# A decoder's state space stage: every third state's product du x B on VectorE instead of GpSimd

## What is computed

```python
xz = x @ W_in
xc, r = jnp.split(xz, 2, axis=-1)
xs = causal_conv(xc, conv_w) + conv_b              # 4 taps
u = silu(xs)
dbc = u @ W_x
delta = softplus(dbc[..., :dtr] @ W_dt + b_dt)
Bm = dbc[..., dtr:dtr + n]                          # n = 16 states
Cm = dbc[..., dtr + n:]
deltaA = jnp.exp(jnp.einsum('bld,dn->lbdn', delta, A))
deltaBu = jnp.einsum('bld,bln->lbdn', delta * u, Bm)
h = dA * h + dBu                                    # along the 256 tokens
y = sum_n h[n] * c[n] + u * D
out = y * silu(r)
return out @ W_out + xs
```

## Time and profile before

| what | value |
|---|---|
| median of 3 runs | 3277.06 us (3275.04 to 3279.24) |
| the profiled execution | 3278.29 us |
| its span | 3276.5 us |
| TensorE busy over the span | 2911.2 us (89%) |
| VectorE busy | 2047.5 us (62%) |
| ScalarE busy | 1527.8 us (47%) |
| GpSimd busy | 1007.0 us (31%) |
| state space stage, first to last scan | 1883.9 to 2523.8 us |

### The profile page before, as it was taken

One profiled execution on the slowest core, in us unless ns is written; L12 is line 12 of the kernel. 1 busy time (PEld: TensorE's weight loads), 2 busy tenths in 40 slices (PEclk: granted clock), 3 DMA queues, 4 the chain that ended last, 5 costly groups with the idle time before them and its releaser, 6 DMA issues. The chain is left out here.

```text
span 3276.5 us, 51834 instructions
## 1 busy us (share of the span) xinstructions
PE 2911.2 (89%) x19136; PEld 1909.8 (58%) x19136; DVE 2047.5 (62%) x2551; ACT 1527.8 (47%) x2911; POOL 1007.0 (31%) x937
## 2 busy tenths in 40 slices
PE   7999688788888888869999899999985999989998
PEld 5666355434444444436666677777763556657776
DVE  4788544589999999670111099999998223324444
ACT  3444211288999998641221276666662111114443
POOL 0000044346666665430000067656666000000000
PEclk9999799889999999889999999999996999989999
DMA  2010322268888888640003111111113611200000
GB/s 87 27 39 26 106 62 69 56 132 168 157 169 168 169 169 181 154 158 14 26 26 125 46 46 53 52 52 52 46 46 101 100 35 38 65 20 14 26 26 27
DMA packets 497941, 256.57 MB, mean 78 GB/s; under 512 B 412112, under 2 KB 449616, under 8 KB 496208
## 3 DMA queue, kind: packets, MB, share of 16 engines
q1 hardware_dynamic: 487456, 247.66, 29.9%
q0 software_dynamic: 10288, 6.29, 1.3%
HBM read 121.65 MB, written 33.69 MB: 47 GB/s over the span
## 5 line engine op out<-in xcount | busy, mean ns | idle before, releaser
L1063 DVE TENSOR_REDUCE xh_top<-xh_seen 128x1 f32<-128x512 f32 (+1 forms) x768 | 632.1, 863 | 59.3 <-PE xh_seen L965 45.5
L1035 ACT ACTIVATE xh_prob<-xh_sc,xh_bias,xh_scale 128x1024 int16<-128x1024 f32 (+1 forms) x512 | 610.0, 1201 | 77.7 <-PE xh_sc L965 73.9
L1929 POOL TENSOR_TENSOR ss_state<-ss_du,ss_b_all 128x1024 f32<-128x1024 f32 x128 | 376.0, 2944 | 264.7 <-PE ss_turned L1649 188.1
L965 PE MATMUL xh_seen<-xh_kT,xh_qT 96*128 96x512 bf16 x1024 | 358.0, 392 | 78.4 <-DVE xh_top L1063 76.0
L1969 DVE TENSOR_TENSOR_SCAN ss_state<-ss_decay,ss_state 128x1024 f32<-128x1024 f32 x128 | 377.4, 2949 | 34.4 <-ACT ss_decay L1828 34.4
L965 PE MATMUL xh_sc<-xh_kT,xh_qT 96*128 96x512 bf16 x1024 | 314.2, 389 | 1.3 <-ACT xh_prob L1035 1.3
L1089 POOL CAST xh_probT<-xh_pairs 128x2048 int16<-128x2048 uint8 x128 | 241.8, 1889 | 17.2 <-DMA xh_pairs<-xh_prob 8.8
L1656 PE MATMUL ss_bank<-ss_xc,hold_w_conv 128*128 128x256 f32 x1024 | 237.7, 388 | 0.7 <-ACT ss_xc L1840 0.7
L965 PEld LDWEIGHTS xh_seen<-xh_kT,xh_qT 96*128 96x128 bf16 x1024 | 90.2, 98 | 240.4 <-DVE xh_top L1063 216.0
L1828 ACT ACTIVATE ss_decay<-ss_delta,ss_a 128x255 f32<-128x255 f32 x512 | 210.7, 496 | 25.9 <-DVE ss_state L1969 25.5
L1656 PEld LDWEIGHTS ss_bank<-ss_xc,hold_w_conv 128*128 128x128 f32 x1024 | 195.8, 195 | 29.0 <-ACT ss_xc L1840 1.1
(11 more groups left out here) (281 smaller groups left out, 4962.4 us busy)
## 6 DMA issues: line engine op xcount, KB each, us to landing
ss_b_all<-ss_states SPq DMA_DIRECT2D x8, 2048.0 KB, 7.2
xa_kT<-xp_kT SPq DMA_DIRECT2D x8, 768.0 KB, 6.0
xh_qT<-xa_qT SPq DMA_DIRECT2D x48, 128.0 KB, 3.3
xh_kT<-xa_kT SPq DMA_DIRECT2D x48, 128.0 KB, 3.3
sa_x<-in_x SPq DMA_DIRECT2D x8, 512.0 KB, 3.7
sa_y<-in_x SPq DMA_DIRECT2D x8, 512.0 KB, 4.7
x_after_self_attention<-sa_y_out SPq DMA_DIRECT2D x8, 512.0 KB, 3.0
xp_x<-x_after_self_attention SPq DMA_DIRECT2D x8, 512.0 KB, 6.6
```

The lines of the kernel that those rows point to most:

```text
L965: ins = pe.matmul(out[:, c * D:(c + 1) * D], qT[s][:, t * P:(t + 1) * P], kT[s][:, at + c * D:at + (c + 1) * D], start=True, stop=True)
L1035: act.activation(out, scores, ACT.Exp, bias=bias[t % RING][:, :], scale=scale[s][:, t:t + 1], accum_out=total[s][:, half, t:t + 1]).then_i ...
L1063: ins = v.tensor_reduce(top[t % RING][:, k:k + 1], scores[:, 0:n], AX.X, ALU.max)\
L1929: g.tensor_tensor(state[k % RING][:, :, :], du[s][:, :, :], spread(b_all[s][:, k, :], KD), ALU.mult)\
```

## The change

The products of states 2, 5, 8, 11 and 14 are issued by VectorE at the end of the slot before their scan; the other eleven stay on GpSimd in their slots. VectorE's products count on a semaphore of their own, `drive_there`, and the scans and SyncE's refill of `b_all` wait on the one or both that concern them. Everything else keeps its place.

```diff
@@ -1472,6 +1472,8 @@
     UNITS = 18
     DECAY_LEAD = 2
     DRIVE_LEAD = 3
+    BY_VECTOR = (2, 5, 8, 11, 14)
+    BY_POOL = [k for k in range(N) if k not in BY_VECTOR]
     SUM_LAG = 2
     CONV_B, OUT_T, X_T, Y0, DT_B, C_T, Y1, Z, XC, SKIP, XC1, GATE, CONV_A = 0, 1, 3, 5, 6, 7, 8, 9, 11, 12, 14, 15, 17
     with Phase(nc, "ss", "right") as p:
@@ -1494,7 +1496,7 @@
         filled = [p.sem(f"filled{i}") for i in range(BANKS)]; freed = [p.sem(f"freed{i}") for i in range(BANKS)]
         b_out = p.sem("b_out"); b_in = p.sem("b_in"); held_in = p.sem("held_in")
         exp_z = p.sem("exp_z"); ln_z = p.sem("ln_z"); delta_ready = p.sem("delta_ready"); du_ready = p.sem("du_ready")
-        decay_ready = p.sem("decay_ready"); drive_ready = p.sem("drive_ready"); scanned = p.sem("scanned")
+        decay_ready = p.sem("decay_ready"); drive_ready = p.sem("drive_ready"); drive_there = p.sem("drive_there"); scanned = p.sem("scanned")
         turn_ready = p.sem("turn_ready"); summed = p.sem("summed"); gated = p.sem("gated")
         y_done = p.sem("y_done"); chain_y = p.sem("chain_y"); waited = p.sem("waited")
         v_waited = p.sem("v_waited")
@@ -1577,6 +1579,10 @@
 
             return q * (2 * N) + s * N + k
 
+        def driven(q, s, k, which):
+
+            return (q * 2 + s) * len(which) + sum(other < k for other in which)
+
         @block.sync
         def _(sp):
             behind.finish(sp)
@@ -1599,7 +1605,8 @@
                     sp.dma_start(slot.rearrange("o (n t) -> (o n) t", t=S), b_rows[:, :]).then_inc(b_out, 16)
                     sp.wait_ge(b_out, ONE + 16 * (n + 2))
                     if post:
-                        sp.wait_ge(drive_ready, ONE + chunk_of(q, s, 0))
+                        sp.wait_ge(drive_ready, ONE + driven(q, s, 0, BY_POOL))
+                        sp.wait_ge(drive_there, ONE + driven(q, s, 0, BY_VECTOR))
                     sp.dma_start(flat(b_all[1 - s][:, :, :]), slot.to_broadcast([P, N * S])).then_inc(b_in, 16)
                 if back:
                     if post:
@@ -1940,9 +1947,9 @@
                         g.tensor_tensor(flat(acc[1 - s][:, :, :]), flat(acc[1 - s][:, :, :]), flat(gate[1 - s][:, :, :]),
                                         ALU.mult).then_inc(gated, 1)
                     if k + DRIVE_LEAD < N:
-                        if back:
+                        if back and k + DRIVE_LEAD in BY_POOL:
                             drive(q, s, k + DRIVE_LEAD)
-                    elif mid:
+                    elif mid and k + DRIVE_LEAD - N in BY_POOL:
                         drive(q + s, 1 - s, k + DRIVE_LEAD - N)
                     if k == 11 and post:
                         inverse_root(g, ln, n - 1)
@@ -1965,9 +1972,19 @@
                 def scan(k):
                     c = chunk_of(q, s, k)
                     v.wait_ge(decay_ready, ONE + c + 1)
-                    v.wait_ge(drive_ready, ONE + c + 1)
+                    if k in BY_VECTOR:
+                        v.wait_ge(drive_there, ONE + driven(q, s, k, BY_VECTOR) + 1)
+                    else:
+                        v.wait_ge(drive_ready, ONE + driven(q, s, k, BY_POOL) + 1)
                     v.tensor_tensor_scan(flat(state[k % RING][:, :, :]), flat(decay[k % RING][:, :, :]),
                                          flat(state[k % RING][:, :, :]), 0.0, ALU.mult, ALU.add).then_inc(scanned, 1)
+
+                def drive(k):
+                    c = chunk_of(q, s, k)
+                    if not (isinstance(q, int) and c < RING):
+                        v.wait_ge(turn_ready, ONE + (c - RING + 1) * TB)
+                    v.tensor_tensor(state[k % RING][:, :, :], du[s][:, :, :], spread(b_all[s][:, k, :], KD), ALU.mult)\
+                        .then_inc(drive_there, 1)
 
                 def add_up(q, s, k):
                     c = chunk_of(q, s, k)
@@ -1988,6 +2005,8 @@
                             add_up(q, s, k - SUM_LAG)
                     elif post:
                         add_up(q - 1 + s, 1 - s, N + k - SUM_LAG)
+                    if back and k + 1 in BY_VECTOR:
+                        drive(k + 1)
                     if k in (8, 10) and post:
                         t, j = ((0, Y0), (1, Y1))[k == 10]
                         if t == 0:
```

## The result

The changed kernel takes 3309.3 us in the median of five runs (3303.0 to 3312.0), the kernel before 3277.1 (3275.0 to 3279.2). The ratio is 1.0093, 95% interval 1.0079 to 1.0107: 30 us more by the ratio, 32 between the medians. The profiled execution took 3303.0 us and is the fastest of the five.

A forecast was written before the change was run, and what follows sets the result against it. VectorE was taken to bound each step in slots 10 to 14, not GpSimd. Middle steps 13.5 us, step 1 2.3, step 0 1.5, last step 2.0: 19.3 us, giving 3297 us, range 3283 to 3312.

The forecast's parts named there:

- Slots 10 to 14 are VectorE's, slots 0 to 9 have slack: Within a step, time added on VectorE in slots 10 to 14 lengthens every step; in slots 0 to 9 it is absorbed.
- +2.7 us a step, made of collisions: Slots 10 to 14: VectorE and GpSimd wait out each other's instructions, so TensorE starts slot 15 2.7 us later each step.
- scan 10 behind drive 12: VectorE's scan 10 still waits out GpSimd's product for state 12; getting in front would shift the step about 2 us.
- drive 11 behind drive 13: Slot 10: VectorE's product 11 waits out GpSimd's product 13, putting scan 11 back 2.95 us.
- Price of a product on VectorE: Each moved product takes 1.22 us on VectorE, 1.26 with the wait of the scan behind it; repeated operand free.
- All steps, 19.3 us: Whole stage: 13.5 us for steps 2 to 6, 2.3 for step 1, 1.5 for step 0, 2.0 for the last.
- the y instructions behind drive 14: Slot 13: after VectorE's product 14, GpSimd's second product goes before the y instructions, which end near 2202.5; scan 14 +2.7 us.
- The clock, "I take next to nothing": TensorE's slow clock at slot 15's start: next to nothing added, but 10 us kept in the range if the stretch doubles.
- The walk through the middle steps: Collisions followed instruction by instruction through one step, +2.7 us each; the favoured case, +12 to +29 us overall, chance 0.68.
- the hidden: Rival: TensorE's chain sets the step and VectorE's added time vanishes in slack, 3277 us; chance 0.11.
- the faster case: Rival: VectorE and GpSimd's mutual exclusion is the bound and VectorE holds it for less time, 3260 us; chance 0.09.
- the dearer one (B): Rival: slow clock doubled, or products in slots 10 and 13 each wait out a whole product; about 3318 us, chance 0.12.

The follow-up runs named there:

- the filled kernels: Extra matmuls in TensorE's wait before slot 15's transposes: seven in the changed kernel, 3294.7 us; four in the kernel before, 3273.0 us.
- the second profile: The changed kernel run and profiled once more with nothing altered, against the kernel before: 3307.3 us, ratio 1.0095.

## Why the prediction was right, and where it was short

- **Slots 10 to 14 are VectorE's, slots 0 to 9 have slack**: shown, by products 2, 5 and 8 costing nothing in steps 3 to 5, and by the moved y.
- **+2.7 us a step, made of collisions**: shown. 2.64 in the profile (2205.46 less 2202.82), 2.6 in the filled kernels. The two neighbours that it hangs on, scan 10 behind drive 12 and drive 11 behind drive 13, were there in both profiles, and moving drive 11 by one place gave the 1.7 back.
- **Price of a product on VectorE**: 1.22 us, repeated operand and all, 1.26 to the next start, as taken.
- **All steps, 19.3 us**: the terms for the ends were too small. Collisions cost 24 to 25 us. Steps 2 to 6 make 13.2 of that (forecast 13.5). Step 0 makes 3.8 us in the second profile (forecast 1.5), step 1 makes 3.1 (forecast 2.3), the last makes 4.1 (forecast 2.0): together 11 us where 5.8 had been taken. One mechanism in the first and last step was missed (VectorE, steps 0 and 7, and GpSimd's product of acc and gate in step 7, in the second profile):

```profile
1952.47 2.02 DVE L1986 TENSOR_TENSOR ss_state<-ss_du,ss_b_all 128x1024 f32<-128x1024 f32 x1
1954.59 4.25 DVE L1979 TENSOR_TENSOR_SCAN ss_state<-ss_decay,ss_state 128x1024 f32<-128x1024 f32 x1
```

```profile
2480.02 2.02 DVE L1986 TENSOR_TENSOR ss_state<-ss_du,ss_b_all 128x1024 f32<-128x1024 f32 x1
2482.14 4.24 DVE L1979 TENSOR_TENSOR_SCAN ss_state<-ss_decay,ss_state 128x1024 f32<-128x1024 f32 x1
```

```profile
2480.92 3.31 POOL L1947 TENSOR_TENSOR ss_acc<-ss_acc,ss_gate 128x1024 f32<-128x1024 f32 x1
```

  The scan behind a product on VectorE must wait for its end, and in that gap (0.1 us in these rows) GpSimd's waiting instruction takes its turn; the scan then stands behind it for a whole product, 4.25 us instead of 2.27. The prediction had seen this for the y instructions behind drive 14, and not for scans. How much of the 5 us it makes isn't told apart.
- **The clock, "I take next to nothing"**: a second term that was too small. It was worth about 4 to 8 us, of the 10 that the range had kept for it. In the second profile slot 15 takes 10.55 us instead of 9.75 in most steps. The forecast tied the clock to the longer waits; that isn't shown. Products 11 and 14 together have the same wait of 3.62 us and 10.5 to 10.7 us for slot 15 in steps 2 to 5, but product 14 alone, with 3.64 us, has 9.4 to 9.7, no more than the kernel before.
- So the forecast was 19.3 and the loss 28 to 32: the time lies in the range near its upper end, 12 us above the value given. The walk through the middle steps was right; that the range held is in part luck, because its upper 10 us were kept for the clock and also had to cover the 5 us of the ends. Of the rivals, the hidden and the faster case are out; of the dearer one (B) the first half, the clock, came true in part, with less than a doubling of the slow stretch.
- The Trainium skill's preference for VectorE in elementwise work ("GPSIMD Engine Reference", Engine selection) holds for the single instruction here, 1.22 against 2.36 us, and says nothing of which engine is the one that is waited for. In this kernel the faster engine was the wrong one.

## What to carry to other kernels

Before work is moved from a slow engine to a fast one, find out in which stretch of the period each engine is the one waited for: in the middle steps, of five equal products three together cost nothing, the fourth alone next to nothing and the fifth alone 2.4 us. They must be tried together too, for here the parts add up to 22 us and the whole is 28 to 32. Where two engines can't run together, a move costs its own time plus whatever is under way on the other when it comes up; a walk through one period from the timeline gave that to a tenth of a microsecond here, but the first and last steps need a walk of their own, and a move by one place can be worth more than the instruction. Look for work without a hurry in the critical stretch: y's normalisation, two slots later, gave 20 us for a change of one number.

## What the runs showed that was not expected

TensorE's clock turns on small waits, but the length of the wait before slot 15 doesn't decide by itself. The kernel before, with 2.4 us, takes 9.7 to 10.1 us for the slot in all the steps 1 to 5. With product 11 alone and 2.3 to 2.5 us of waiting it took 9.7 in three of them, 8.45 and 7.97 in the others. With the moved y in the changed kernel, 2.8 to 2.9 us meant 8.1 to 8.4 four times and 9.7 once. The changed kernel, with 3.6 to 3.7 us, took 8.5 to 10.8. What the rule is stays open. That the slow stretch can be bought off is shown: 1.7 us of idle work a step made the kernel before 6.6 us faster.

A waiting instruction of GpSimd gets its turn in a gap of 0.1 us between two dependent instructions of VectorE, 0.03 us in the row at 2201.96. That makes a dependence between two neighbours on VectorE cost up to a whole instruction of GpSimd: 4.25 and 4.32 us for scans that take 2.27 alone.
